# The edges' keys and packed words worked out by GpSimd instead of VectorE

## The reference

```python
h = relu(layernorm(x))
msgs = h[src]
out = h @ root + bias
for r in range(8):
    mask = (edge_type == r)
    sums = segment_sum(msgs * mask[:, None], dst, num_segments=1250)
    cnt = segment_sum(mask, dst, num_segments=1250)
    out = out + (sums / maximum(cnt, 1)[:, None]) @ weight[r]
u = out
z = concatenate([u, h], axis=1) @ w_gate + b_gate
y = x + tanh(u) * z + h * (1 - z)
```

## Time and profile before

| what | value |
|---|---|
| runs shown | 1405.66, 1406.08 and 1414.51 us |
| median | 1406.08 us |
| profiled execution, first to last instruction (span) | 1407.7 us |
| PE busy | 1291.5 us, 92% of the span |
| DVE busy | 952.5 us, 68% |
| POOL busy | 754.8 us, 54% |
| ACT busy | 409.0 us, 29% |
| chain that ended last | PE 61%, DVE 13%, DMA 10%, issue 7%, POOL 4% |

### The profile page before, as it was taken

One profiled execution on the slowest core, in us unless ns is written; L12 is line 12 of the kernel. 1 busy time (PEld: TensorE's weight loads), 2 busy tenths in 40 slices (PEclk: granted clock), 3 DMA queues, 4 the chain that ended last, 5 costly groups with the idle time before them and its releaser, 6 DMA issues.

```text
span 1407.7 us, 20144 instructions
## 1 busy us (share of the span) xinstructions
PE 1291.5 (92%) x6205; PEld 651.6 (46%) x6205; DVE 952.5 (68%) x1260; ACT 409.0 (29%) x501; POOL 754.8 (54%) x837
## 2 busy tenths in 40 slices
PE   2978899999999999999998999998999989786898
PEld 1434344444444445555554445454445445343565
DVE  6889678366565667775675577646666778765777
ACT  5344123214132422321332043223222323432000
POOL 2423088786878426686687558664756464320000
PEclk9998899999999999999999999999999999998999
DMA  6442125215224348777875887769889977648872
GB/s 220 154 173 101 44 52 156 69 45 171 54 59 122 114 158 277 238 237 247 277 209 161 292 267 246 238 210 305 279 254 303 312 230 240 204 138 248 239 226 90
DMA packets 112355, 269.44 MB, mean 191 GB/s; under 512 B 22558, under 2 KB 23061, under 8 KB 112268
## 3 DMA queue, kind: packets, MB, share of 16 engines
q1 hardware_dynamic: 78284, 185.88, 40.2%
q0 software_dynamic: 33984, 82.40, 20.4%
HBM read 203.66 MB, written 87.30 MB: 207 GB/s over the span
## 4 chain that ended last, share of the span: by engine, by line
PE 61%; DVE 13%; DMA 10%; issue 7%; POOL 4%; ACT 2%; DVEq 1%; SPq 1%; POOLq 1%; ACTq 0%
PE ps L1320 52%; PE ps L1278 8%; DMA early<-y_rows,pair 7%; DVE W L937 2%; DMA early<-u_rows 1%; POOL onehot L641 1%; DVE hT L990 1%; DMA W<-in_L_gnn_weight_dram 1%; POOL early L633 1%; DVE hT L985 1%; PE ps L1313 1%; POOL pair L623 1%; DVE early L1147 1%; DVE early L1069 1%; DVE early L1163 1%
## 5 line engine op out<-in xcount | busy, mean ns | idle before, releaser
L1320 PE MATMUL ps<-W,hT 128*128 128x512 f16 (+2 forms) x4740 | 1076.0, 385 | 13.0 <-DVE W L937 13.0
L1320 PEld LDWEIGHTS ps<-W,hT 128*128 128x128 f16 (+2 forms) x4740 | 479.9, 104 | 537.8 <-issue 43.4
L633 POOL DMA_INDIRECT early<-y_rows,pair x200 | 242.1, 1211 | 194.5 <-PE ps L1281 152.4
L606 POOL DMA_INDIRECT table_rows<-edges,table_i x160 | 240.5, 1503 | 100.6 <-issue 100.6
L1278 PE MATMUL ps<-early,onehot 128*125 x800 | 205.9, 385 | 26.6 <-POOL onehot L641 13.1
L641 POOL TENSOR_SCALAR onehot<-iota_d,pair 128x125 f16<-128x125 f16 x185 | 159.9, 864 | 64.2 <-DMA early<-y_rows,pair 58.2
L766 ACT ACTIVATE yhl<-early 128x512 f16<-128x512 f32 x120 | 75.3, 628 | 355.3 <-DVE early L1069 194.2
L937 DVE SCALAR_TENSOR_TENSOR W<-W,wsc 128x2048 f16<-128x2048 f32 x62 | 146.5, 2364 | 13.8 <-ACT W L716 13.7
L1278 PEld LDWEIGHTS ps<-early,onehot 128*125 x800 | 106.8, 137 | 100.4 <-issue 46.6
L716 ACT ACTIVATE W<-W,wsc 128x2048 f16<-128x2048 f32 x62 | 122.6, 1990 | 50.9 <-DVE wsc L932 20.3
L683 ACT ACTIVATE peek_out<-W 128x1024 bf16<-128x1024 f32 x80 | 84.2, 1052 | 94.7 <-DMA W<-in_L_gnn_weight_dram 72.7
(11 more groups left out here) (184 smaller groups left out, 756.0 us busy)
## 6 DMA issues: line engine op xcount, KB each, us to landing
y_rows<-yhl SPq DMA_DIRECT2D x144, 256.0 KB
W<-in_L_gnn_weight_dram SPq DMA_DIRECT2D x31, 1024.0 KB, 7.4
early<-u_rows SPq DMA_DIRECT2D x52, 448.0 KB
u_rows<-early SPq DMA_DIRECT2D x50, 448.0 KB
W<-in_L_gnn_w_gate_dram SPq DMA_DIRECT2D x8, 1024.0 KB, 8.3
early<-in_x_dram SPq DMA_DIRECT2D x9, 512.0 KB, 4.5
hs_rows<-early SPq DMA_DIRECT2D x9, 512.0 KB, 3.2
u_rows<-yhl SPq DMA_DIRECT2D x18, 256.0 KB
```

Of the source, the lines that this page charges most:

```text
L606: pool.indirect_dma_start(out=table_rows, out_offset=bass.IndirectOffsetOnAxis(ap=at_i[:, c:c + 1], axis=0), in_=packed[0:EP, c:c + 1], in ...
L633: pool.indirect_dma_start(out=G[:, b, :], out_offset=None, in_=y_rows[i], in_offset=bass.IndirectOffsetOnAxis(ap=idx[:, b, :], axis=0), bo ...
L1320: last = nc.tensor.matmul(ps[0:rows, n % 4, :], hT[:, m, v_h, k, n0:n0 + rows], Wh[MAT[w][c]][:, v_w, k, :], start=(first and v_h + v_w == ...
```

## The change

POOL works out the keys and packed words in place of DVE. The call moves from DVE's n = 2 to POOL's program between `split_low(1)` and `split_low(2)`. [...] DVE's version had 27 instructions and POOL's has 41: 4 copies, 21 tensor_scalar and 16 tensor_tensor, all of 125x160, each followed by a wait for its own end (all but the last). DVE waits for the new semaphore `keys_ready` ahead of each `scan_part`.

```diff
-    KEYS_AT, SCAN_AT, TOTALS_AT, BOUNDS_AT = 2, {4: 0, 7: 1, 10: 2, 12: 3}, 14, 16
+    SCAN_AT, TOTALS_AT, BOUNDS_AT = {4: 0, 7: 1, 10: 2, 12: 3}, 14, 16
...
+            def step(ins):
+                steps[0] += 1
+                ins.then_inc(s["pool_step"], 1)
+                pool.wait_ge(s["pool_step"], steps[0])
+
+            def edge_keys():
+                pool.wait_ge(s["edges_loaded"], 48)
+                step(pool.tensor_copy(dst_f, dst_i))
+                step(pool.tensor_copy(typ_f, typ_i))
+                step(pool.tensor_copy(src_f, src_i))
+                step(pool.tensor_scalar(grp, dst_f, -(DT - 1) / 2, 1.0 / DT, ALU.add, ALU.mult))
+                step(pool.tensor_scalar(grp, grp, ROUND, None, ALU.add))
+                step(pool.tensor_scalar(grp, grp, -ROUND, None, ALU.add))
+                step(pool.tensor_scalar(at_f, grp, -float(DT), 1.0, ALU.mult, ALU.add))
+                step(pool.tensor_tensor(dst_f, dst_f, at_f, ALU.add))
+                step(pool.tensor_scalar(at_f, typ_f, float(N), None, ALU.mult))
+                step(pool.tensor_tensor(src_f, src_f, at_f, ALU.add))
+                step(pool.tensor_scalar(at_f, grp, float(SWEEPS[0][1]), None, ALU.mult))
+                step(pool.tensor_tensor(key[0:EP, :], at_f, typ_f, ALU.add))
+
+                def add(to, scale, of):
+                    step(pool.tensor_scalar(at_f, of, float(scale), None, ALU.mult))
+                    step(pool.tensor_tensor(to, to, at_f, ALU.add))
+
+                for i in range(1, NS):
+                    (p0, p1), (r0, r1) = SWEEPS[i - 1:i + 1]
+                    step(pool.tensor_scalar(later_sweep, typ_f, float(r0), None, ALU.is_ge))
+                    add(src_f, -(r0 - p0) * N, later_sweep)
+                    add(key[0:EP, :], SPAN[i][0] - SPAN[i - 1][0] - (r0 - p0), later_sweep)
+                    if r1 - r0 != p1 - p0:
+                        step(pool.tensor_tensor(later_sweep, later_sweep, grp, ALU.mult))
+                        add(key[0:EP, :], (r1 - r0) - (p1 - p0), later_sweep)
+                step(pool.tensor_scalar(src_f, src_f, float(P), None, ALU.mult))
+                step(pool.tensor_tensor(src_f, src_f, dst_f, ALU.add))
+                pool.tensor_copy(packed[0:EP, :], src_f).then_inc(s["keys_ready"], 1)
+                steps[0] += 1
...
             for i in range(NJ):
                 split_low(i)
+                if i == LEAD - 1:
+                    edge_keys()
                 if 2 <= i <= SQ + 1:
                     scan_factors(i - 2)
...
-            def edge_keys():
-                dve.wait_ge(s["edges_loaded"], 48)
-                nc.vector.tensor_copy(src_f, src_i)
...
             def scan_part(b):
                 g0, g1 = b * NG // SQ, (b + 1) * NG // SQ
+                dve.wait_ge(s["keys_ready"], 1)
...
-                if n == KEYS_AT:
-                    edge_keys()
```

More of the change, by code:

```diff
@@ L336, in gated_rgcn_preln @@
             "w_hi", "w_lo", "t_ready",
-            "factors_ready", "scan_ready", "totals_done", "ltile_ready", "bounds_done", "bounds_ready", "ranked", "pos_ready",
+            "keys_ready", "factors_ready", "scan_ready", "totals_done", "ltile_ready", "bounds_done", "bounds_ready", "ranked", "pos_ready",
             "table_clear", "table_filled", *(f"scattered{b}" for b in range(SQ)), "table_loaded", "table_ready",
@@ L576, in _ @@
             pool.memset(hT[:, A21:A22 + 1, :, :, (HT - 1) * P + PAD:HT * P], 0.0).then_inc(s["pad_clear"], 1)
+            steps = [0]
+            def step(ins):
[31 more added lines that the diff above has]
+                steps[0] += 1
             def split_low(i):
```

## The result

The changed kernel takes 1413.3 us (median of 20 runs, 1402.4 to 1422.2) where the kernel before takes 1406.1 us (median of 20 runs, 1399.9 to 1414.5). The ratio of the two is 1.0037, with a 95% interval of 1.0019 to 1.0054. So the change costs 5.2 us by the ratio (2.7 to 7.6), and 7.2 us by the medians. The forecast was 1414, slower but within 1%.

The account below looks back on a forecast made before the run. The edge-sorting stage was taken as bound by DVE. A 12.8 us later low half of tile 2 against 7.5 us of relief lost 5.3 us, plus 2.9 for the clock: +8.2 on 1406.1, 1414.3 us, range 1401 to 1424.

Parts of the forecast that it names:

- The forecast case: POOL's keys end after PE wants tile 2; PE's stall outweighs DVE's relief: +8.2 us, 1414.3 us; chance 52%.
- The start of the keys: POOL's first cast begins when the edge loads land, taken as 19 us from the short packets in the queue.
- The 41 steps: POOL's dependent key instructions with their waits between them, ahead of tile 2's low half: 25.8 us, between 18.5 and 34.4.
- The lock: DVE's four low halves of the first weight exclude POOL's two-input steps amid the keys, adding 9.1 us.
- K: The end of POOL's keys, ahead of tile 2's low half: 53.9 us, between 46.6 and 62.5.
- The clock: PE's granted clock near 0.5 behind the stall at tile 2 slows its matmuls and transpositions: 2.9 us.
- PE is next at n = 3: Without keys on DVE, scan part 0 waits for PE's n = 3: 58.9 against 66.4, at most 7.5 us won.
- 1 to 1 from scan part 0 to the end: A shift at scan part 0 carries unchanged through n = 20 to the end: 8.2 us stay.
- The prediction's last sign of being wrong: The forecast is wrong if the shift at n = 20 is not the shift at the end.
- Rival (a): POOL's steps cost as much as its dearest rows, 34.4 us in all: +16.8 us, 1423 us; chance 17%.
- rival (b): POOL's keys are cheap and done, or nearly, before PE wants tile 2: faster, 1401 us; chance 18%.
- rival (c): POOL shuts DVE out through all its keys, so the first weight's low half waits: +13.0 us, 1419 us; chance 10%.

Follow-up runs that it names:

- second execution: The changed kernel unaltered, run and profiled again: n = 20 at 182.40 us, span 1419.1 us, median 1413.6 us, ratio 1.0031 to the kernel before.
- split version with gated memsets: split version with the scan factors' memsets moved ahead of tile 2, POOL first waiting for the first weight's scale; ratio 0.9957 to the kernel before.
- split version: Changed kernel with only the first 12 steps left on POOL, the rest on DVE at n = 2 in fused form; ratio 0.9962 to the kernel before.

## Why the prediction was right

The forecast case came: POOL's keys do not fit the hole, PE waits for them at tile 2, and DVE's relief pays for a part of it. The sum was 3 us too high at scan part 0 (+8.2 forecast, +5.05 measured), from two terms. The interval of the ratio, 2.7 to 7.6 us, lies below 8.2 and inside the forecast's own range of +4 to +13. That the median came within 1 us of the forecast is luck: the medians happen to stand further apart (7.2 us) than either the ratio (5.2) or n = 20 (5.5).

- **The start of the keys**, 19 us by the short packets: 19.58, and 18.95 in the second execution. Right.
- **The 41 steps**, 25.8 us: 32.6 us in all less 7.4 of stretching is 25.2. Its parts were off and made up for each other: tensor_tensor 0.52 and not 0.48, tensor_scalar 0.61 (two of them 0.32) and not 0.49, copies 0.32 and not 0.4, and gaps of 0.08 and not 0.15. So this term is right by luck in its parts. The one-hot row, 0.61 us for 125 elements, showed the same price as it stood, and scaled up to 160 elements, 0.73, it was too dear. The Trainium skill's rule of roughly line rate for one-input operations (GPSIMD Engine Reference, Engine selection), for which the prediction took 0.32 us, did not hold for 19 of the 21, at 0.61 us; it fitted the two with a multiplication and an addition. (By the prediction's own terms the sum under that rule is 22.2 us and not 22.3, and the slope gives a tensor_tensor 0.49 us and not 0.48; neither matters.)
- **The lock**, 9.1 us: 7.4. Each of four steps waited 1.6 to 1.9 us for a low half of 2.3, since it began some time into it. In turn DVE lost 0.6 us of the 2 allowed.
- **K**, 53.9: 52.2, so the stall ended 11.1 us later than the 43.25 of before and not 12.8. This is 1.7 of the 3 us.
- **The clock**, 2.9 us: the granted clock was 0.50 behind the stall as foreseen, but the loss was smaller. From the low half's transposition to the end of n = 3 it took 15.7 us against 14.3, so 1.4 us. The 36 matmuls took 8.94 us and not 10.09 as in the earlier trace rows. This is the other 1.5 us. The windows of the changed kernel, with the granted clock as the third figure from the end:

```profile
54.00:56.00 2.00, 1.64 (x10) 1.14 (x11) 0.57 (x1) 0.00 (x0) 2.00 (x2) 0.50 0.04 8
...
56.00:60.00 4.00, 4.00 (x17) 1.73 (x16) 1.11 (x3) 0.60 (x1) 4.00 (x4) 0.85 0.61 208
```

The prediction priced this by the stall, and the other runs do not bear that out. The same 36 matmuls took 9.64 us behind a wait of 8.10 us, 10.48 behind 9.26, 8.97 behind 10.56, 10.06 behind 10.58, 8.94 behind 12.01 and 9.04 behind 21.60. And five kernels with the same short wait of 1.58 us as the kernel before took 8.96 to 9.30 us, where that one and the split version with gated memsets took 7.93. The split version, for one:

```profile
43.54 1.04 PE L1262 MATMUL ps<-ident_h,early 128*128 128x128 f16 x8 [1.58 <-POOL early L604]
44.37 9.12 PE L1335 MATMUL ps<-W,hT 128*128 128x512 f16 x36
```

So the clock's loss at this place was between nothing and 2.6 us on these matmuls, and its size did not follow the length of the wait. That the longer stall caused the changed kernel's 1.4 us is therefore not shown. In the split version it cost little: the transposition was 0.4 us longer, and behind the keys DVE came later than PE.

- **PE is next at n = 3**, so that DVE can win 7.5 us at most: confirmed in the changed kernel, where DVE waits for n = 3 ahead of scan part 0, which starts 1.4 us behind its end. The 58.9 of the prediction and the 11.1 and 1.4 us measured make 71.4, and scan part 0 stands at 71.47. No version reached the 7.5 us as a gain: the best at unmoved scans won 5.8, and in it, as in the kernel before, scan part 0 started 7.3 us behind the end of DVE's keys, so DVE was still the later one.
- **1 to 1 from scan part 0 to the end**: +5.05 became +5.5 at n = 20 and +5.2 by the ratio. Over eleven kernels it holds within the intervals in all but one. The prediction's last sign of being wrong, a shift at n = 20 that is not the shift at the end, did come up in the first profiled execution (+5.5 and -1.1); the repetition and the 20 runs answer it.
- **Rival (a)** took 0.73 us for the tensor_scalar, nearer to the 0.61 than the forecast's 0.49 on most of them, and 0.24 for the gap, which was 0.08; **rival (b)** failed on the lock and the price together; **rival (c)** did not come, since DVE got its turn between POOL's dependent steps, 0.08 us apart, each time. Its mechanism exists: eight memsets without such gaps kept DVE out for 11.50 us.

## What to carry to other kernels

An idle engine's hole is worth its length less what its neighbour locks it out of, and work put into it must end before the engine's next duty in somebody else's chain: here 32.6 us went into 25, of which 3.5 had passed when the edges landed. Put into such a hole only what fits (12 of 41 steps, and memsets placed beside two-input operations), and leave the rest where it takes fewer instructions. Compare stages by a fixed event in the trace, such as the start of n = 20, when a later stage varies by more than the change is worth.

## What the runs showed of the hardware

- On GpSimd, undisturbed, a tensor_scalar of 125x160 f32 took 0.32 to 0.33 us for multiply and add in either order (0.39 once), 0.61 to 0.64 with one operation (0.70 and 0.72 once each), and 0.75 to 0.78 for add and add or is_ge and multiply. A tensor_tensor took 0.52 us and a cast 0.32.
- A one-input VectorE operation of 128x3 waited 11.50 us through eight GpSimd memsets in a row, and in another kernel with the same memsets 5.98 us through the first half of them. With the memsets held back until behind it, it took 0.45. The two-input ones of 128x2048 beside the same memsets took 2.3 us as always.
- Between two dependent GpSimd steps 0.08 us passed, and VectorE's waiting operation got its turn there every time, four times of four in the changed kernel.
- Behind a wait of 1.58 us TensorE's 36 matmuls of 128x512 took 7.93 us in two kernels, at a granted clock of 1.00, and 8.96 to 9.30 us in five others, where it first stood near 0.50; behind waits of 8.10 to 21.60 us they took 8.94 to 10.48 us, in no order of length.
